# Head output of the first sequence moved among the last attention pairs, and the router worked out for each sequence by itself

## Chip, cores and metric

The kernel runs on one NeuronCore of one Trainium2 chip. The metric is the device time of one execution in microseconds (us), from the median of several runs. Engines are named as the profile names them: PE is TensorE's matmul, PEld its weight load, DVE is VectorE, ACT is ScalarE, POOL is GpSimd and SP issues DMAs.

## What is computed

A two-layer model on x of shape (2, 256, 256), two sequences of 256 tokens. Each layer adds a cross attention over a context of 4096 tokens, then a second block, then a feed-forward block. This case is about the end of the second layer: self attention with 16 heads of 64 (8 causal, 8 not), then a mixture of 8 experts. The last parts of the reference:

```python
out = jnp.concatenate([out_ar, out_diff], axis=1)
out = out.transpose(0, 2, 1, 3).reshape(b, l, H * D_HEAD)
return out @ Wo                       # head output, added to x
...
def _router(x, expert_embeddings):
    dot2 = jnp.einsum('bsh,eh->bse', x, expert_embeddings).reshape(n, E)
    vals, idx = jax.lax.top_k(dot2, K)                  # K = 2 of E = 8
    masked = jnp.full_like(dot2, -jnp.inf).at[rows, idx].set(vals)
    return jax.nn.softmax(masked, axis=-1)
expert_capacity = math.ceil(n_tokens / E * CAP_FACTOR)  # 64
weights = _router(x, expert_embeddings)
ones = (weights > 0).astype(weights.dtype)
cap_ones = jnp.where(jnp.cumsum(ones, axis=0) <= expert_capacity, ones, 0.0)
caw = weights * cap_ones
vals, idx = jax.lax.top_k(caw.T, expert_capacity)
tokens = x_flat[idx.reshape(-1)].reshape(E, expert_capacity, hidden)
inter = jax.nn.relu(jnp.einsum('ech,eih->eci', tokens, first_linear))
out = jnp.einsum('eci,ehi->ech', inter, second_linear) * vals[:, :, None]
final = jnp.zeros((n_tokens, hidden), x.dtype).at[index].add(out.reshape(-1, hidden))
```

The count of chosen tokens (`cumsum`) runs over all 512 tokens, so the second sequence's slots depend on the first sequence's choices. The first sequence's don't depend on the second.

## The kernel before

The 512 tokens lie in four tiles of 128 (X[:, 0] to X[:, 3]). Tiles 0 and 1 are the first sequence (b = 0), 2 and 3 the second. Each engine has one program, written out by hand in order, and the engines meet only at semaphores: an instruction that waits holds up all that stands behind it on its engine. DVE also waits for itself (`done()`) wherever an operation reads the result of the one before it.

**The last pairs of the self attention.** 16 heads of 2 sequences make 16 pairs of heads; pairs 0 to 7 are the first sequence's. PE's loop over pairs does `head_scores(pair + 2)`, two `turn_weights` (transposes, L2618), and `weigh_heads(pair - 1)` (L2642). Before a `turn_weights`, both DVE (`scale_exps`, L1806) and POOL (L763) scale the exponentials. Its result is copied out by DVE (`copy_weights`, L1814) for the even head and by ACT (L1160) for the odd one, and `weigh_heads` reads those copies. The contexts are copied into OT by DVE (`copy_contexts`, L1820) or ACT (`copy_contexts_a`, L1147).

**Head output.** After `weigh_heads(15)` PE multiplies OT by WOM for the four tiles (`linear_rows`, L2186, 8 matmuls a tile, each of float32 and so shown as 2 passes). DVE adds each tile to X (L1843), takes mean and variance (L1419, L1402), adds the epsilon (L1388), has ACT take the square root (L905, which needs the table of the square root), inverts it (L1381) and writes the normalised HLE (`centred`, L1423), all once for each sequence.

**Router.** PE turns HLE (`turn_half`, L2158), ACT copies it (L1019), PE multiplies by the expert embeddings (logits, L2699). With the logits of both sequences in PSUM, DVE makes the choice for four tiles at once (L1858 to L1873), ACT takes one Exp (L1167), DVE ends the choice (L1876 to L1880, CHOSENB for PE), PE counts (L2709), DVE gives slots (L1885, L1888) and builds the selection SEL for each tile (L1891). PE gathers the tokens by a matmul of HLE with SEL that sums over the four tiles (L2717), while DVE works out the shares (L1894 to L1903) and SELW, the weighted selection (L1907, four tiles). PE then waits for the whole SELW and for XG, which ACT copies out (L1170), and goes on with `turn_chosen` (L2729) and the experts (L2738, L2748, L2757) and the combination (L2765), which are left as they are. `keep_awake` (L2166) are matmuls whose result nobody reads; they stand in PE's order where it would wait.

Of the kernel before, what the change touches and what calls it, by code (L numbers as in the profile page):

```python
# [16 lines left out]
P = 128  # L17
# [128 lines left out]
def build(nc, t):  # L146

    ctx = ExitStack()
    with ctx:
# [6 lines left out]
        def f32(at, n):  # L156
            return arena[:, at:at + n]
# [197 lines left out]
        R = [f32(34816 + 32 * i, 32).rearrange("p (t e) -> p t e", e=E) for i in range(12)]  # L355
# [4 lines left out]
        R1 = [f32(35200 + 4 * i, 4) for i in range(8)]  # L360
# [298 lines left out]
        def _(pool):  # L659
# [529 lines left out]
        def _(dve):  # L1189
# [632 lines left out]

            for n in range(4):
                row_maxima(n)
# [3 lines left out]
            for pair in range(16):  # L1828
# [6 lines left out]
                if pair + 1 < 16:  # L1835
                    invert_sums(pair + 1)
                    scale_exps(n + 2)
                copy_weights(n)
                if pair + 1 < 16:
                    scale_exps(n + 3)  # L1840
            copy_contexts(15)
            for b in range(B):
                add_to_x("f_out", 4, lambda i: nc.vector.tensor_tensor(X[:, i, :], X[:, i, :], psum[:, i, 0:256], ALU.add),  # L1843
                         2 * b, 2 * b + 2)
                deviation(first=2 * b, last=2 * b + 2)
                for i in (2 * b, 2 * b + 1):
                    centred(HLE, X, i).then_inc(h_ready, 1)
            dve.wait_ge(on["g_logits"], 1)
            logits, hot1, hot2, weights, chosen, slot, pick = R[0], R[1], R[2], R[3], R[4], R[5], R[6]
            best1, best2, gap, egap, den, share1, share2 = R1[0], R1[1], R1[2], R1[3], R1[4], R1[5], R1[6]  # L1850
            less8 = const("experts").unsqueeze(1).broadcast_to((P, TT, E))

            def over_e(ap):
                return ap.unsqueeze(2).broadcast_to((P, TT, E))

            raw = psum[:, 0, 0:TT * E].rearrange("p (t e) -> p t e", t=TT)
            for best, hot, seen in ((best1, hot1, raw), (best2, hot2, logits)):
                mark(nc.vector.tensor_reduce(best, seen, AX.X, ALU.max))  # L1858
                done()
                mark(nc.vector.tensor_tensor(pick, seen, over_e(best), ALU.is_equal))  # L1860
                done()

                mark(nc.vector.tensor_tensor(pick, pick, less8, ALU.mult))
                done()
                mark(nc.vector.tensor_reduce(R1[7], pick, AX.X, ALU.min))
                done()
                mark(nc.vector.tensor_tensor(hot, less8, over_e(R1[7]), ALU.is_equal))
                done()
                if best is best1:
                    mark(nc.vector.scalar_tensor_tensor(out=logits, in0=hot, scalar=-3.0e38, in1=raw,  # L1870
                                                        op0=ALU.mult, op1=ALU.add))
                    done()
            nc.vector.tensor_tensor(gap, best2, best1, ALU.subtract).then_inc(on["g_logits"], 1)  # L1873

            dve.wait_ge(on["g_logits"], 3)
            mark(nc.vector.scalar_tensor_tensor(out=pick, in0=over_e(egap), scalar=0.0, in1=hot2,  # L1876
                                                op0=ALU.is_gt, op1=ALU.mult))
            done()
            nc.vector.tensor_tensor(CHOSENB, hot1, pick, ALU.add).then_inc(on["g_chosen"], 1)
            mark(nc.vector.tensor_tensor(chosen, hot1, pick, ALU.add))  # L1880
            done()
            dve.wait_ge(on["g_cum"], 1)
            cum = psum[:, 1, 0:TT * E].rearrange("p (t e) -> p t e", t=TT)

            mark(nc.vector.scalar_tensor_tensor(out=slot, in0=cum, scalar=float(CAP), in1=chosen,  # L1885
                                                op0=ALU.is_le, op1=ALU.mult))
            done()
            mark(nc.vector.tensor_tensor(slot, slot, cum, ALU.mult))  # L1888
            done()
            for i in range(TT):  # L1890
                nc.vector.tensor_tensor(SEL[:, i], slot[:, i, :].unsqueeze(2).broadcast_to((P, E, CAP)),  # L1891
                                        const("slots").unsqueeze(1).broadcast_to((P, E, CAP)), ALU.is_equal)\
                  .then_inc(on["g_sel"], 1)
            mark(nc.vector.tensor_scalar(den, egap, 1.0, None, ALU.add))  # L1894
            done()
            mark(nc.vector.reciprocal(share1, den))
            done()
            mark(nc.vector.tensor_tensor(share2, egap, share1, ALU.mult))
            mark(nc.vector.tensor_tensor(hot1, hot1, over_e(share1), ALU.mult))
            done()  # L1900
# [962 lines left out]
```

## Time and profile before

| | before |
|---|---|
| times | 911.25, 912.66, 912.73 us, median 912.66 |
| the profiled execution's own time | 912.04 us |
| span of its trace | 910.2 us |
| PE / DVE / ACT / POOL busy, share of the span | 96% / 67% / 52% / 15% |
| chain that ended last: PE, DVE, ACT | 82%, 10%, 3% |
| TensorE's granted clock, mean | 0.996 of full speed |

The time of the profiled execution is 1.8 us more than the span, which runs from the first to the last instruction that the trace counts as work. Times in the rows further down are from the span's start. A name such as L2186 is a line of the kernel as printed above. A PE busy share of 96% says only that a matmul was almost always under way, keep-awake matmuls among them; whether it was work that the end depends on is read from the chain of waits.

### The profile page before, as it was taken

Reading aid. Unit: us, or ns where it says so; the run is one execution under the profiler, and the core shown is the slowest. Engines: PE = TensorE matmul, PEld = TensorE weight load, DVE = VectorE, ACT = ScalarE, POOL = GpSimd, SP = SyncE. Lnnn points to the kernel's source line nnn. Section 1 sums busy time; section 2 is a strip of 40 time slices with the busy share of each in tenths; the row PEclk is TensorE's granted clock in tenths of the full one; section 3 lists DMA queues with packets and bytes.
Section 4 is the critical chain, followed back from the end, with each engine's and each line's share of the span. In section 5 each row is a group of like instructions: output and inputs, shape, how many; then the busy total and the mean of one; then the engine's idle time right before and its main releaser. Section 6 shows DMA issues by size and latency. Waiting matters only on the chain.

```text
span 910.2 us, 15328 instructions
## 1 busy us (share of the span) xinstructions
PE 874.1 (96%) x6037; PEld 519.5 (57%) x6037; DVE 609.7 (67%) x1068; ACT 474.4 (52%) x958; POOL 136.2 (15%) x141
## 2 busy tenths in 40 slices
PE   7799999999999999999999999999999999999998
PEld 3355544444556665555554578755784784656745
DVE  5879677777886556888883389886724327469352
ACT  4242566777776556777778962314411310668221
POOL 5434011111000000000000071010100005336100
PEclk9899999999999999999999999999999999999999
DMA  9978934546433311333533260084643805000000
GB/s 354 276 202 193 209 110 124 147 125 159 115 71 71 81 36 36 70 71 71 137 123 132 94 249 2 1 277 140 231 185 134 329 1 186 1 1 1 1 1 24
DMA packets 55081, 108.49 MB, mean 119 GB/s; under 512 B 5408, under 2 KB 38176, under 8 KB 49824
## 3 DMA queue, kind: packets, MB, share of 16 engines
q1 hardware_dynamic: 51568, 97.26, 37.6%
q10 hardware_dynamic: 3440, 10.22, 3.7%
q8 instruction: 50, 0.82, 0.4%
q14 instruction: 23, 0.19, 0.1%
HBM read 93.58 MB, written 13.89 MB: 118 GB/s over the span
## 4 chain that ended last, share of the span: by engine, by line
PE 82%; DVE 10%; ACT 3%; issue 2%; DMA 2%; POOL 0%; ACTq 0%; SPq 0%; DVEq 0%
PE psum L2019 14%; PE psum L2001 13%; PE psum L1967 12%; PE psum L2421 6%; PE psum L2449 6%; PE psum L1944 6%; PE psum L2553 5%; PE psum L1934 4%; PE psum L2186 3%; DVE arena L1501 3%; PE psum L2618 2%; DVE arena L1252 2%; PE psum L2603 2%; PE psum L2173 2%; PE psum L2642 1%
## 5 line engine op out<-in xcount | busy, mean ns | idle before, releaser
L1252 DVE TENSOR_REDUCE arena<-psum 128x1 f32<-128x1024 f32 x256 | 301.1, 1219 | 102.4 <-PE psum L1967 101.9
L823 ACT ACTIVATE arena<-psum 128x512 f32<-128x512 f32 x512 | 263.6, 604 | 67.8 <-PE psum L2001 66.5
L1967 PE MATMUL psum<-arena 96*128 96x512 bf16 x512 | 153.2, 381 | 10.0 <-DMA arena<-qparts 4.8
L2001 PE MATMUL psum<-arena 99*128 99x256 bf16 x1024 | 155.1, 274 | 3.9 <-ACT arena L814 1.7
L2019 PE MATMUL psum<-arena 128*32 128x256 f32 x2048 | 137.0, 385 | 0.0
L2001 PEld LDWEIGHTS psum<-arena 99*128 99x128 bf16 x1024 | 80.6, 97 | 98.6 <-ACT arena L823 36.7
L2019 PEld LDWEIGHTS psum<-arena 128*32 128x32 f32 x2048 | 53.4, 109 | 74.2 <-ACT arena L823 30.7
L1934 PE MATMUL psum<-arena 128*128 128x512 f32 x128 | 61.7, 609 | 6.0 <-DMA arena<-ctxT 5.5
L682 POOL TENSOR_TENSOR arena<-arena 128x512 bf16<-128x512 f32 x34 | 41.3, 1214 | 174.5 <-DVE arena L1238 171.8
L1967 PEld LDWEIGHTS psum<-arena 96*128 96x128 bf16 x512 | 48.9, 98 | 29.1 <-DVE arena L1252 11.4
L1944 PE MATMUL psum<-arena 128*128 128x256 f32 x256 | 63.8, 386 | 0.0
L2449 PE MATMUL psum<-arena 128*128 128x256 f32 x256 | 57.9, 379 | 0.0
L2421 PE MATMUL psum<-arena 128*128 128x512 f32 x128 | 57.2, 595 | 0.0
L1944 PEld LDWEIGHTS psum<-arena 128*128 128x128 f32 x256 | 48.5, 194 | 13.1 <-issue 4.8
L2449 PEld LDWEIGHTS psum<-arena 128*128 128x128 f32 x256 | 47.5, 190 | 5.8
L806 ACT ACTIVATE arena<-psum 128x512 f32<-128x512 f32 x32 | 19.1, 598 | 52.4 <-PE psum L1944 52.4
L2173 PE MATMUL psum<-arena 128*128 128x256 f32 (+1 forms) x208 | 44.1, 366 | 0.4 <-ACT arena L1032 0.2
L800 ACT ACTIVATE arena<-psum,arena 128x512 bf16<-128x512 f32 x32 | 22.0, 686 | 42.9 <-PE psum L1934 29.4
L702 POOL MEMSET arena<- 128x4 f32 x1 | 0.1, 106 | 290.1 <-PE psum L2019 290.1
L2553 PE MATMUL psum<-arena 128*128 128x512 f32 x96 | 42.8, 595 | 0.0
L2173 PEld LDWEIGHTS psum<-arena 128*128 128x128 f32 x208 | 37.1, 190 | 7.5 <-issue 1.4
L1934 PEld LDWEIGHTS psum<-arena 128*128 128x128 f32 x128 | 24.0, 195 | 28.3 <-issue 21.6
(269 smaller groups left out, 1014.1 us busy)
## 6 DMA issues: line engine op xcount, KB each, us to landing
kparts<-arena SPq DMA_DIRECT2D x32, 384.0 KB, 3.0
arena<-kparts SPq DMA_DIRECT2D x32, 384.0 KB, 5.2
arena<-kparts SPq DMA_DIRECT2D x32, 256.0 KB, 5.7
arena<-mask SPq DMA_DIRECT2D x8, 1024.0 KB, 5.2
arena<-ctx SPq DMA_DIRECT2D x2, 4096.0 KB, 17.5
arena<-ctxT SPq DMA_DIRECT2D x14, 512.0 KB, 6.0
arena<-ctxT ACTq DMA_DIRECT2D x10, 512.0 KB, 15.4
arena<-mask ACTq DMA_DIRECT2D x4, 1024.0 KB, 9.9
```

Source lines behind the costliest of these rows:

```text
L682: nc.gpsimd.tensor_tensor(parts[:, 2, :], rest, parts[:, 1, :], ALU.subtract).then_inc(k_low, 1)
L823: nc.scalar.activation(PR[step % 4][:, pair * CH:(pair + 1) * CH], exp_bank(step, pair), ACT.Exp)\
L1252: nc.vector.tensor_reduce(MX[g % 2][:, col:col + 1], unit_banks(n).rearrange("p b n -> p (b n)"), AX.X, ALU.max).then_inc(s_maxed, 1)
L1934: last = nc.tensor.matmul(ring_bank(slot), WK[:, k, f * P:(f + 1) * P], CTX[n % SLOTS][:, k, :], start=(k == 0), stop=(k == CT - 1))
L1944: last = nc.tensor.matmul(ring_bank(slot)[:, v * 256:(v + 1) * 256], CTX[n % SLOTS][:, k, (2 * i + v) * P:(2 * i + v + 1) * P], WV[:, k, : ...
L1967: last = nc.tensor.matmul(out, q, KST[g % 2][0:ROWS, quarter, j, half * CH:(half + 1) * CH], start=True, stop=not masked, skip_group_check ...
L2001: last = nc.tensor.matmul(heads[:, u, :], KST[gg % 2][0:KROWS, kc // 8, j, kc % 8 * P:(kc % 8 + 1) * P], QST[0:KROWS, b, G * g + j, :], st ...
L2019: last = nc.tensor.matmul(PV[32 * j:32 * (j + 1), :], V_flat[:, at:at + 32], PR[step % 4][:, j * S:(j + 1) * S], start=(kc == 0), stop=(kc ...
L2173: last = nc.tensor.matmul(out, weights[:, k, m * P:m * P + width], xs[k], start=(k == 0), stop=(k == n - 1))
L2421: last = nc.tensor.matmul(psum[:, unit % 3, :], QC[:, c, w * P:(w + 1) * P], CTXT[w // 2][:, c, n * 512:(n + 1) * 512], start=(c == 0), st ...
L2449: last = nc.tensor.matmul(psum[:, 6, 0:256], PT1[:, k * P:(k + 1) * P], CTXK[w // 2][:, k, :], start=(k == 0), stop=(k == KC - 1), skip_gr ...
L2553: last = nc.tensor.matmul(out, HTF[:, c, i * P:(i + 1) * P], WQKV[which][:, c, half * HALF:(half + 1) * HALF], start=(c == 0), stop=(c == ...
```

## The change

- **Head output of the first sequence.** `heads_out(0)` and `heads_out(1)` stand in PE's loop at pair 14, ahead of `weigh_heads(13)`, and the wait for the first eight pairs' contexts with them. DVE adds them to X at pair 15, ahead of `copy_weights(30)`.
- **Normalisation.** For both sequences the inverse square root is now one power operation on POOL (`power`) instead of ACT's root and DVE's reciprocal.
- **Router for each sequence.** Choice, count, slots, selection and shares are done on two tiles at a time, first for b = 0, then for b = 1. DVE's order becomes: centre 0, last context copy, choose 0, add tiles 2 and 3, ask for the power, slots 0, centre 1, select 0, share 0, choose 1, slots 1, select 1, share 1, then SELW for all four tiles.
- **PE's order** is given at the end of the diff. The keep-awake matmuls go from 8, 3, 14 and 5 to 8, 3, 1 and 5.
- **R and R1**, the router's small tiles, lie elsewhere, since OT is still in use when the first choice is made.

```diff
-        R = [f32(34816 + 32 * i, 32).rearrange("p (t e) -> p t e", e=E) for i in range(12)]
+        R = [f32(55168 + 32 * i, 32).rearrange("p (t e) -> p t e", e=E) for i in range(12)]
...
             nc.gpsimd.tensor_copy(UPPER, const("upper")).then_inc(built, 1)
+            powers[0] += B
+            for b in range(B):
+                power(2 * b, 2 * b + 2)
...
             for b in range(B):
-                root(2 * b, 2 * b + 2)
+                two = slice(2 * b, 2 * b + 2)
                 copy_turned_half(b, HTF)
-            act.wait_ge(on["g_logits"], 2)
-            signal(nc.scalar.activation(R1[3], R1[2], ACT.Exp), "g_logits")
+                act.wait_ge(on["g_logits"], 3 * b + 2)
+                signal(nc.scalar.activation(R1[3][:, two], R1[2][:, two], ACT.Exp), "g_logits")
             for c in range(CT):
...
+            def add_heads(first, last):
+                add_to_x("f_out", 4, lambda i: nc.vector.tensor_tensor(X[:, i, :], X[:, i, :], psum[:, i, 0:256], ALU.add),
+                         first, last)
...
                     scale_exps(n + 2)
+                if pair == 15:
+                    add_heads(0, 2)
+                    ask_root(0, 2)
                 copy_weights(n)
...
-            copy_contexts(15)
-            for b in range(B):
-                add_to_x("f_out", 4, lambda i: nc.vector.tensor_tensor(X[:, i, :], X[:, i, :], psum[:, i, 0:256], ALU.add),
-                         2 * b, 2 * b + 2)
-                deviation(first=2 * b, last=2 * b + 2)
...
+            def centre_for_experts(b):
+                take_power()
                 for i in (2 * b, 2 * b + 1):
                     centred(HLE, X, i).then_inc(h_ready, 1)
...
+            def choose(b):
+                two = slice(2 * b, 2 * b + 2)
+                dve.wait_ge(on["g_logits"], 3 * b + 1)
+                raw, rest, mine = of_bank(0, b), logits[:, two], pick[:, two]
+                for best, hot, seen in ((best1, hot1, raw), (best2, hot2, rest)):
+                    mark(nc.vector.tensor_reduce(best[:, two], seen, AX.X, ALU.max))
...
+                nc.vector.tensor_tensor(gap[:, two], best2[:, two], best1[:, two], ALU.subtract).then_inc(on["g_logits"], 1)
+                dve.wait_ge(on["g_logits"], 3 * b + 3)
+                mark(nc.vector.scalar_tensor_tensor(out=mine, in0=over_e(egap[:, two]), scalar=0.0, in1=hot2[:, two],
+                                                    op0=ALU.is_gt, op1=ALU.mult))
+                done()
+                nc.vector.tensor_tensor(CHOSENB[:, two], hot1[:, two], mine, ALU.add).then_inc(on["g_chosen"], 1)
+                mark(nc.vector.tensor_tensor(chosen[:, two], hot1[:, two], mine, ALU.add))
+                done()
+            def number_slots(b):
+                two = slice(2 * b, 2 * b + 2)
+                dve.wait_ge(on["g_cum"], b + 1)
+                cum = of_bank(1, b)
+                mark(nc.vector.scalar_tensor_tensor(out=slot[:, two], in0=cum, scalar=float(CAP), in1=chosen[:, two],
+                                                    op0=ALU.is_le, op1=ALU.mult))
+                done()
+                mark(nc.vector.tensor_tensor(slot[:, two], slot[:, two], cum, ALU.mult))
+                done()
+            def select(b):
+                for i in (2 * b, 2 * b + 1):
+                    nc.vector.tensor_tensor(SEL[:, i], slot[:, i, :].unsqueeze(2).broadcast_to((P, E, CAP)),
+                                            const("slots").unsqueeze(1).broadcast_to((P, E, CAP)), ALU.is_equal)\
+                      .then_inc(on["g_sel"], 1)
+            def share(b):
+                two = slice(2 * b, 2 * b + 2)
+                mark(nc.vector.tensor_scalar(den[:, two], egap[:, two], 1.0, None, ALU.add))
...
+            centre_for_experts(0)
+            copy_contexts(15)
+            choose(0)
+            add_heads(2, 3)
+            add_heads(3, 4)
+            ask_root(2, 4)
+            number_slots(0)
+            centre_for_experts(1)
+            select(0)
+            share(0)
+            choose(1)
+            number_slots(1)
+            select(1)
+            share(1)
...
+            def heads_out(i):
+                linear_rows(psum[:, i, 0:256], tok(OT, i), WOM, False, "f_out")
+            def logits(b):
+                turned()
+                for i in (2 * b, 2 * b + 1):
+                    for c in range(CT):
+                        last = nc.tensor.matmul(psum[:, 0, i * E:(i + 1) * E], HTF[:, c, i * P:(i + 1) * P], EMB[:, c, :],
+                                                start=(c == 0), stop=(c == CT - 1))
+                last.then_inc(on["g_logits"], 1)
+            def count_chosen(b):
+                pe.wait_ge(on["g_chosen"], b + 1)
+                for i in (2 * b, 2 * b + 1):
+                    for j in range(i + 1):
+                        last = nc.tensor.matmul(psum[:, 1, i * E:(i + 1) * E], UPPER if j == i else ONESB,
+                                                CHOSENB[:, j, :], start=(j == 0), stop=(j == i))
+                last.then_inc(on["g_cum"], 1)
+            def gather(i):
+                pe.wait_ge(on["g_sel"], i + 1)
+                for c in range(CT):
+                    last = nc.tensor.matmul(psum[:, 2 + c, :], HLE[:, i, c * P:(c + 1) * P],
+                                            SEL[:, i].rearrange("p e s -> p (e s)"), start=(i == 0),
+                                            stop=(i == TT - 1), skip_group_check=True)
+                    if i == TT - 1:
+                        last.then_inc(on["g_xg"], 1)
...
+                if pair == 14:
+                    for n in range(8):
+                        contexts_copied(n)
+                    heads_out(0)
+                    heads_out(1)
                 weigh_heads(pair - 1)
             weigh_heads(15)
-            pe.wait_ge(pv_copied, NG + contexts_by(7, True))
-            pe.wait_ge(on["f_pv_copied"], contexts_by(7, False))
-            for i in range(TT):
-                if i == 2:
-                    pe.wait_ge(pv_copied, NG + contexts_by(15, True))
-                    pe.wait_ge(on["f_pv_copied"], contexts_by(15, False))
-                if i == TT - 1:
-                    turn_half(HLE, 0, 4 * TT)
-                linear_rows(psum[:, i, 0:256], tok(OT, i), WOM, False, "f_out")
+            turn_half(HLE, 0, 4 * TT)
+            for n in range(8, 16):
+                contexts_copied(n)
+            heads_out(2)
             pe.wait_ge(on["const_loaded"], 32)
-            for b in range(B):
-                if b:
-                    keep_awake(6, 8)
-                    turn_half(HLE, 1, 4 * TT)
-                    keep_awake(6, 3)
-                turned()
-                for i in (2 * b, 2 * b + 1):
-                    for c in range(CT):
-                        last = nc.tensor.matmul(psum[:, 0, i * E:(i + 1) * E], HTF[:, c, i * P:(i + 1) * P], EMB[:, c, :],
-                                                start=(c == 0), stop=(c == CT - 1))
-            last.then_inc(on["g_logits"], 1)
+            logits(0)
+            heads_out(3)
+            pe.wait_ge(built, 13)
+            count_chosen(0)
+            keep_awake(6, 8)
+            turn_half(HLE, 1, 4 * TT)
+            keep_awake(6, 3)
+            logits(1)
             pe.wait_ge(on["x_ready"], 5 * TT)
-            keep_awake(6, 14)
-            pe.wait_ge(on["g_chosen"], 1)
-            pe.wait_ge(built, 13)
-            for i in range(TT):
-                for j in range(i + 1):
-                    last = nc.tensor.matmul(psum[:, 1, i * E:(i + 1) * E], UPPER if j == i else ONESB,
-                                            CHOSENB[:, j, :], start=(j == 0), stop=(j == i))
-            last.then_inc(on["g_cum"], 1)
+            gather(0)
+            gather(1)
+            keep_awake(6, 1)
+            count_chosen(1)
             keep_awake(6, 5)
-            for i in range(TT):
-                pe.wait_ge(on["g_sel"], i + 1)
-                for c in range(CT):
-                    last = nc.tensor.matmul(psum[:, 2 + c, :], HLE[:, i, c * P:(c + 1) * P],
-                                            SEL[:, i].rearrange("p e s -> p (e s)"), start=(i == 0),
-                                            stop=(i == TT - 1), skip_group_check=True)
-                    if i == TT - 1:
-                        last.then_inc(on["g_xg"], 1)
+            gather(2)
+            gather(3)
             pe.wait_ge(on["g_selw"], TT)
```

## Rows read from the trace of the kernel before

**Rows 1.** Chain that ended last, last 68 us: start us, us, what.
```profile
864.94 1.74 PE psum L2166 x8
868.32 1.07 PE psum L2699 x8
872.78 0.42 PE psum L2709 x10
874.50 7.13 PE psum L2717 x16
```

**Rows 2.** Timeline of PE: start us, us, engine, line, operation, tile, count, [idle before].
```profile
849.63 10.23 PEld L2186 LDWEIGHTS psum<-arena 128*128 128x128 f32 x48 [0.38 <-ACT arena L1147]
863.99 0.95 PE L2699 MATMUL psum<-arena 128*128 128x8 f32 x8
882.43 0.20 PEld L2738 LDWEIGHTS psum<-arena 128*64 128x64 f32 x4 [0.17 <-ACT arena L1170]
```

**Rows 3.** Timeline of the last pairs, PE and VectorE, columns as in the timeline above.
```profile
841.13 1.13 PE L2618 MATMUL psum<-arena 128*128 128x128 f32 x8
845.43 0.63 PEld L2642 LDWEIGHTS psum<-arena 128*64 128x64 f32 x8 [0.17 <-issue]
846.45 0.42 PEld L2618 LDWEIGHTS psum<-arena 128*128 128x128 f32 x4 [0.39 <-DVE arena L1806]
847.14 0.69 DVE L1814 COPY arena<-psum 128x512 f32<-128x512 f32 x1 [0.83 <-PE psum L2618]
847.75 1.49 PEld L2642 LDWEIGHTS psum<-arena 128*64 128x64 f32 x16 [0.17 <-issue]
849.75 0.42 DVE L1820 COPY arena<-psum 128x256 f32<-128x256 f32 x1 [1.92 <-PE psum L2642]
```

**Rows 4.** Timeline of VectorE: adding a head output tile, and one tile's statistics earlier.
```profile
853.39 0.42 DVE L1843 TENSOR_TENSOR arena<-arena,psum 128x256 f32<-128x256 f32 x1 [3.22 <-PE psum L2186]
572.67 0.42 DVE L1483 TENSOR_TENSOR arena<-arena,psum 128x256 f32<-128x256 f32 x1 [1.49 <-PE psum L2186]
573.81 0.15 DVE L1390 TENSOR_SCALAR arena<-arena 128x1 f32<-128x1 f32 x1
```

**Rows 5.** Timeline: powers on POOL and what follows them, and a normalisation before.
```profile
598.89 1.28 DVE L1570 SCALAR_TENSOR_TENSOR arena<-arena 128x1024 f32<-128x1024 f32 x1
599.05 1.52 POOL L737 TENSOR_TENSOR arena<-arena 128x1 f32<-128x1 f32 x1 [2.94 <-DVE arena L1388]
668.20 0.17 DVE L1388 TENSOR_SCALAR arena<-arena 128x2 f32<-128x2 f32 x1
669.18 0.74 DVE L1423 TENSOR_SCALAR arena<-arena 128x256 f32<-128x256 f32 x2 [0.21 <-POOL arena L737]
866.23 0.73 DVE L1423 TENSOR_SCALAR arena<-arena 128x256 f32<-128x256 f32 x2
```

**Rows 6.** Timeline of VectorE: selection, shares, weighted selection.
```profile
873.75 2.50 DVE L1891 TENSOR_TENSOR arena<-arena 128x512 f32<-128x512 f32 x4
876.16 0.16 DVE L1894 TENSOR_SCALAR arena<-arena 128x4 f32<-128x4 f32 x1
877.10 0.19 DVE L1903 TENSOR_TENSOR arena<-arena 128x32 f32<-128x32 f32 x1
877.32 2.50 DVE L1907 TENSOR_TENSOR arena<-arena 128x512 f32<-128x512 f32 x4
```

**Rows 7.** Timeline of ACT: loading the table for the Exp.
```profile
868.28 1.28 ACT L1167 ACT_TABLE_LOAD   x1
```

**Rows 8.** Stretches early on: from:to, length, busy PE PEld DVE ACT POOL, PEclk, DMA.
```profile
37.50:42.30 4.80, 0.00 (x0) 0.00 (x0) 3.62 (x5) 1.26 (x2) 3.35 (x3) 0.77 0.99 230
42.30:46.50 4.20, 4.19 (x10) 2.80 (x11) 2.80 (x4) 0.00 (x0) 0.91 (x2) 0.50 0.77 275
46.90:47.30 0.40, 0.40 (x3) 0.31 (x2) 0.27 (x1) 0.00 (x0) 0.00 (x1) 0.96 1.34 287
97.86:99.52 1.66, 0.00 (x1) 0.01 (x1) 0.00 (x0) 1.15 (x3) 0.00 (x0) 1.00 1.01 201
```

More of the change, by code:

```diff
@@ L359, in build @@
         CHOSENB = b16(44576 + P, TT * E).rearrange("p (t e) -> p t e", e=E)
-        R1 = [f32(35200 + 4 * i, 4) for i in range(8)]
+        R1 = [f32(55552 + 4 * i, 4) for i in range(8)]
         assert 47120 + N_CONSTS <= 48144
@@ L1840, in _ @@
                     scale_exps(n + 3)
-            copy_contexts(15)
-            for b in range(B):
-                add_to_x("f_out", 4, lambda i: nc.vector.tensor_tensor(X[:, i, :], X[:, i, :], psum[:, i, 0:256], ALU.add),
-                         2 * b, 2 * b + 2)
-                deviation(first=2 * b, last=2 * b + 2)
+            logits, hot1, hot2, weights, chosen, slot, pick = R[0], R[1], R[2], R[3], R[4], R[5], R[6]
+            best1, best2, gap, egap, den, share1, share2 = R1[0], R1[1], R1[2], R1[3], R1[4], R1[5], R1[6]
@@ L1849, in _ @@
[L1849 to L1858, printed above, removed]
+            def choose(b):
[5 more added lines that the diff above has]
+                    done()
+                    mark(nc.vector.tensor_tensor(mine, seen, over_e(best[:, two]), ALU.is_equal))
+                    done()
+                    mark(nc.vector.tensor_tensor(mine, mine, less8, ALU.mult))
+                    done()
+                    mark(nc.vector.tensor_reduce(R1[7][:, two], mine, AX.X, ALU.min))
+                    done()
+                    mark(nc.vector.tensor_tensor(hot[:, two], less8, over_e(R1[7][:, two]), ALU.is_equal))
+                    done()
+                    if best is best1:
+                        mark(nc.vector.scalar_tensor_tensor(out=rest, in0=hot1[:, two], scalar=-3.0e38, in1=raw,
+                                                            op0=ALU.mult, op1=ALU.add))
+                        done()
+                nc.vector.tensor_tensor(gap[:, two], best2[:, two], best1[:, two], ALU.subtract).then_inc(on["g_logits"], 1)
+                dve.wait_ge(on["g_logits"], 3 * b + 3)
+                mark(nc.vector.scalar_tensor_tensor(out=mine, in0=over_e(egap[:, two]), scalar=0.0, in1=hot2[:, two],
+                                                    op0=ALU.is_gt, op1=ALU.mult))
@@ L1864, in _ @@
                 done()
-                mark(nc.vector.tensor_reduce(R1[7], pick, AX.X, ALU.min))
+                mark(nc.vector.tensor_tensor(slot[:, two], slot[:, two], cum, ALU.mult))
                 done()
-                mark(nc.vector.tensor_tensor(hot, less8, over_e(R1[7]), ALU.is_equal))
-                done()
[L1869 to L1880, printed above, removed]
@@ L1894, in _ @@
[L1894 to L1900, printed above, removed]
-            mark(nc.vector.tensor_tensor(hot2, hot2, over_e(share2), ALU.mult))
-            done()
-            mark(nc.vector.tensor_tensor(weights, hot1, hot2, ALU.add))
@@ L1904, in _ @@
-            done()
+            def select(b):
[6 more added lines that the diff above has]
+                mark(nc.vector.tensor_scalar(den[:, two], egap[:, two], 1.0, None, ALU.add))
+                done()
+                mark(nc.vector.reciprocal(share1[:, two], den[:, two]))
+                done()
+                mark(nc.vector.tensor_tensor(share2[:, two], egap[:, two], share1[:, two], ALU.mult))
+                mark(nc.vector.tensor_tensor(hot1[:, two], hot1[:, two], over_e(share1[:, two]), ALU.mult))
+                done()
+                mark(nc.vector.tensor_tensor(hot2[:, two], hot2[:, two], over_e(share2[:, two]), ALU.mult))
+                done()
+                mark(nc.vector.tensor_tensor(weights[:, two], hot1[:, two], hot2[:, two], ALU.add))
+                done()
```

20 lines of the change are left out of this document (5 added, 15 removed).

## The prediction

> **What bounds the kernel now.** I first read the page's engine shares: PE is busy for nearly the whole span. That alone says little, since keep-awake matmuls count as busy. So next comes the chain of waits over the last 68 us. Up to the head output it is PE at work. Then it leaves real work: keep-awake matmuls (8 in 1.74 us), logits of the second sequence from 868.32, 3.4 us of small VectorE operations with one Exp between them, the count at 872.78, the selection, and the gather from 874.50 [rows 1]. Behind the gather it is PE's own work to the end. What can be won is therefore the time in which PE waits between the head output and the gather. Then I read the timeline of PE and VectorE over 841 to 883, in which every step below has its row. The point at which both kernels can be compared is the first weight load of the experts, now at 882.43 [rows 2]; all behind it is unchanged. The start is 845.43, where `weigh_heads(13)` begins [rows 3].
>
> **Prices.** A pass of the head output takes 0.2135 us (48 weight loads over 10.23, [rows 2]), so a tile of 16 passes 3.42. `weigh_heads` takes 1.02 (845.43 to 846.45), two of them in a row 1.88 (847.75 to 849.63, the start of the next line) [rows 2, 3]. Two `turn_weights` without a wait between them take 1.13 [rows 3]. Now the last two take 1.30 (846.45 to 847.75), because VectorE and POOL scale late; with 6.8 us of head output ahead of them they no longer wait. Logits of a sequence: 0.95 on PE [rows 2]. From the start of the logits to the count: 4.46 (868.32 to 872.78); from the count to the first gather 1.72 [rows 1]. A gather of two tiles: 8 passes of 0.43, 3.43 (half of the sixteen in 7.13, less the modelled tail) [rows 1].
>
> **Part 1, head output at pair 14.** All adds are to PE's clock of now.
> - Eight waits for contexts stand ahead of `heads_out(0)`. The waits are all met long before, so they cost PE's sequencer only. Four such waits stand before a `weigh_heads`, whose row shows 0.17 idle by issue [rows 3]; twice that, 0.34, is the upper bound, nothing the lower. I take 0.15: start 845.58.
> - Two tiles to 852.42, `weigh_heads(13)` 853.44, two turns 854.57, two `weigh_heads` **856.45**.
> - What VectorE gets ahead of `copy_weights(30)`: its add of tile 1 comes 0.34 behind PE (853.39 against 849.63 + 3.42) [rows 2, 4], at 852.76. From an add to the request for the power one tile takes 1.14 (572.67 to 573.81) [rows 4], the second tile's statistics about 0.43 more: request at 854.33, done by 854.5. The copy takes 0.69 [rows 3] and ends at 855.2. `weigh_heads(15)` wants it at 855.5. So this move past `copy_weights(30)` costs nothing, but by only 0.3 us; if VectorE is later than that, every tenth beyond goes on PE's path.
> - ACT's copy of the odd head stays behind the same transposes as now; it isn't moved.
>
> **Part 2, the power on POOL.** From the request to `centred`, ACT's way and the reciprocal took 0.64 now; POOL's takes 0.98 (668.20 to 669.18) [rows 5]. POOL is idle in this stretch. For the first sequence: 854.33 + 0.98 + 0.74 = 856.1, before `turn_half(0)` wants it at 856.45, so it is hidden (cover 0.4). For the second it is on the path, +0.34. The upper bound is the power that took 1.52 while VectorE ran an operation of 1.28 us on two arena operands [rows 5], 0.8 more than the usual 0.70; here VectorE has two operations of 0.19 there, each with one operand in PSUM, and I take 0.98. This row bears out a rule of the Trainium skill (SBUF — State Buffer, section "SBUF: two separate sides"): VectorE and GpSimd share a port pair, which an operation of VectorE with two SBUF inputs holds to its end while GpSimd is blocked. By that rule alone, with such an operation beside it, the second power would cost 0.8 more; the sum doesn't use it. ACT no longer changes tables; the load of 1.28 us for the Exp (the one for the root is alike) began at 868.28 and was over at 869.56, 3.2 us ahead of the count, which stands a few tenths behind the Exp [rows 1, 7]. Taking both away brings nothing.
>
> **Part 3, the router in halves.** Twelve small operations of the choice are issued twice, the two of the slots and the six of the shares too: 20 more instructions on VectorE, at half the size. An operation on 32 columns takes 0.19, on 4 columns 0.16 [rows 6], so half the size saves about 0.01 each, 0.13 in a choice. So the halves nearly double the time that VectorE spends on the router.
> - `turn_half(0)` from 856.45. `copy_contexts(15)` comes 0.12 behind the last `weigh_heads` and takes 0.42 [rows 3]; then `heads_out(2)` can start, at 857.03, the turn (0.57) is done as well. Ends 860.45. Logits 0 to 861.40, `heads_out(3)` to 864.82.
> - Choice 0 runs beside `heads_out(3)`: count at 860.45 + 4.46 - 0.13 = 864.78. Both sides meet, nothing waits. Count about 0.2.
> - The price of the order: tiles 2 and 3 are added behind choice 0. Tile 2 is ready at 860.8 and waits for VectorE to 864.85. Then each tile passes through add, statistics, aggregate with waits for itself, 1.14 each [rows 4]: request at 867.13, centred from 868.11, and 2.09 from there to logits 1 (866.23 to 868.32) [rows 1, 5]: 870.20. Had tile 2 been taken first, about 0.8 would go.
> - Logits 1 to 871.15, gather of tiles 0 and 1 to 874.58, one keep-awake 0.22 (1.74 / 8, [rows 1]), 874.80. Choice 1 is there at 870.20 + 4.33 = 874.53: hidden by the gather. VectorE before it: centred to 868.85, selection 1.25 (half of 2.50), shares 1.11 (876.16 to 877.32, less 0.05) [rows 6], 871.2: free when the logits come. So here the halves pay: 3.43 of gather lie where 14 keep-awakes were.
> - Count at 874.80, gather of tiles 2 and 3 from + 1.72 = 876.52 to **879.95**. Now the gather ends at 874.50 + 6.86 = 881.36 [rows 1]. Gain there 1.4.
> - But VectorE: selection 1 starts 0.75 before the gather (873.75 against 874.50) [rows 1, 6], 875.77, ends 877.02; shares 1 878.13; the four SELW 2.50 [rows 6]: 880.63. `turn_chosen` waits for all four. Now SELW ends at 879.82, hidden by 1.5 us of gather; then it would be the last, by 0.7. `turn_chosen(0)` from 880.68, the expert load after 1.07 (881.36 to 882.43): **881.75**.
>
> **Sum.** 882.43 - 881.75 = 0.7 us. Against the profiled execution's own time: 912.04 - 0.7 = 911.3. The median of the runs, 912.66, is 0.6 above that execution, so I forecast **912.0** for the median. Most of the 3.4 us of router that becomes hidden is lost again: 0.7 by SELW, about 1 by the later second normalisation, the rest by waits that the keep-awakes only covered.
>
> **Rivals.**
> - **The gather stays last.** VectorE's waits for itself are shorter, or the contexts' waits cost nothing, so SELW is ready before the gather ends. For it: VectorE needs to be only 0.7 faster over 20 operations and four waits, and the serial add of tiles 2 and 3 is priced from a row of another stage. Against: each price is from a row. The gain is then the 1.4 at the gather's end, and up to 2.5 if the serial adds take 0.5 each less: 910.2 to 911.3, in the middle 910.7. Chance 0.2.
> - **Eaten up.** POOL's power takes 1.52 beside VectorE (+0.5), the waits 0.34 (+0.2), halves are no shorter (+0.2), `copy_weights(30)` comes late. Gain about nothing, 912.7 (to 913.3). Chance 0.17.
> - **The clock falls, slower.** After the count of sequence 0 PE has 8 keep-awakes, to 865.05 + 1.74 = 866.8, and then nothing until `turn_half(1)` at 868.11 + 0.53 = 868.6: a pause of 1.85 us; now keep-awakes and work fill almost all of it. In this trace a pause of 1.66 left the clock full, one of 4.80 had it fall to half (1.2 of 2.4 GHz), and half it stayed for 4.6 us after work had begun again, 42.30 to 46.90 [rows 8]. It decides from a pause nearer to the second than to the first. If the clock falls, the next 4.6 us do 2.3 of work: 2.3 lost, net +1.6: 914.3. 1.85 lies close to the harmless row, so 0.05. More generally slower by other late steps (several tenths each of parts 1 and 3 in a row) 0.03.
> - **It doesn't do what it says**, as when PE reaches `heads_out(0)` with contexts not copied: those of pairs 0 to 7 are copied long before pair 14. No chance worth a number.
>
> **How the numbers follow.** Forecast (gain 0.3 to 1.6) 0.55, gather last 0.2, eaten up 0.17, slower 0.08. The range takes in the first three with the scatter of the runs (1.5 us between lowest and highest): 910.1 to 913.6. A measurement of this kernel can tell about 0.2%, 1.8 us, from no change. Faster by more than that needs most of the second case or a median that falls well: 0.2. Slower by more: 0.08, the clock and late steps, 0.1 with scatter. The same: 0.7.
>
> **What would show it.** PE at `turn_half(0)` near 856.4 with no gap in front of `weigh_heads(15)`; `heads_out(3)` directly followed by the count; request to `centred` 0.98 for both sequences; a PE pause of near 1.9 us ahead of `turn_half(1)` with PEclk 1.00; VectorE's last SELW later than the last gather matmul by about 0.7, `turn_chosen` released by VectorE; the expert load 0.7 earlier. It is wrong if `copy_weights(30)` releases PE, if small operations on 16 columns differ much from those on 32, or if SELW isn't last.

## The result, and the profile after

| | before | after |
|---|---|---|
| median of 22 runs | 913.02 us | 914.77 us |
| lowest, highest | 911.25, 914.36 | 912.05, 916.08 |
| profiled execution's own time, span | 912.04, 910.2 | 914.01, 912.1 |
| TensorE's granted clock, mean | 0.996 | 0.994 |

The ratio is 1.0017 with a 95% interval of 1.0010 to 1.0024: the changed kernel is slower, by 1.75 us between the medians and 1.6 us by the ratio, a little less than 0.2%. The forecast was 0.7 us faster. The runs after are spread in an odd way: two of the 22 took 912.1 us at a mean clock of 0.996, two took 912.6 and 913.2 at 0.994, and the other 18 lie at 914.0 to 916.1 with a clock of 0.993 or 0.994. The profiled execution is one of the 18.

In the kernel after, `linear_rows` is L2225, `turn_half` L2197, `keep_awake` L2205, the logits L2702, the count L2710, the gather L2717, `turn_chosen` L2780, the first products of the experts L2789; on VectorE `centred` is L1426, the selection L1912, SELW L1946. First the windows over the router in the trace after, in the form of [rows 8]: from:to, length, busy time of PE, PEld, DVE, ACT and POOL, then PEclk.

```profile
866.50:868.40 1.90, 0.17 (x1) 0.00 (x0) 1.20 (x7) 0.00 (x0) 0.69 (x1) 1.00 0.00 0
868.40:869.50 1.10, 1.06 (x6) 0.71 (x7) 1.10 (x3) 0.18 (x1) 0.00 (x0) 0.83 0.00 0
869.50:871.00 1.50, 1.50 (x8) 1.08 (x6) 1.16 (x7) 0.41 (x1) 0.00 (x0) 0.50 0.00 0
871.00:873.00 2.00, 2.00 (x7) 1.48 (x8) 0.65 (x4) 0.00 (x0) 0.00 (x0) 0.50 0.04 8
873.00:875.00 2.00, 2.00 (x4) 0.82 (x3) 1.46 (x10) 0.20 (x1) 0.00 (x0) 0.50 0.02 4
875.00:876.00 1.00, 1.00 (x2) 0.34 (x1) 0.40 (x3) 0.00 (x0) 0.00 (x0) 0.52 0.00 0
876.00:877.00 1.00, 1.00 (x4) 0.42 (x3) 0.00 (x0) 0.00 (x0) 0.00 (x0) 1.00 0.00 0
```

PEclk is the third number from the end. It is still 1.00 while PE pauses (0.17 us of work in 1.90), falls just after work has begun again, stays at 0.50, which is 1.2 of 2.4 GHz, from about 869 to 876, and is full again after. PE reads as busy all through: half speed looks like work. PE's timeline says what ran there:

```profile
868.44 0.78 PE L2197 MATMUL psum<-arena 128*128 128x128 f32 x4 [1.77 <-DVE arena L1426]
870.25 1.71 PE L2702 MATMUL psum<-arena 128*128 128x8 f32 x8
871.82 5.73 PE L2717 MATMUL psum<-arena 128*128 128x512 f32 x8
877.60 0.32 PE L2710 MATMUL psum<-arena 128*128 128x8 bf16 x7
879.19 3.70 PE L2717 MATMUL psum<-arena 128*128 128x512 f32 x8 [0.17 <-DVE arena L1912]
880.75 2.50 DVE L1946 TENSOR_TENSOR arena<-arena 128x512 f32<-128x512 f32 x4
883.30 1.09 PE L2780 MATMUL psum<-arena 128*128 128x128 f32 x8 [0.41 <-DVE arena L1946]
884.32 1.94 PE L2789 MATMUL psum<-arena 128*64 128x512 f32 x8
```

The brackets of the first line give the pause, 1.77 us, and who ended it: VectorE's `centred` for the second sequence. The logits (L2702) took 1.71 instead of 1.07 for the same eight passes [rows 1], and the gather of tiles 0 and 1 took 5.73 where the same work on tiles 2 and 3 at full clock takes 3.70. That gather hid the second choice in the forecast; now it delays the count, to 877.4.

So that traces can be compared although their earlier stages differ by some tenths of a us, the text below measures one **distance**: from the start of `turn_weights(28)`, the transposes whose wait for POOL is 0.67 or 0.68, to the first weight load of the experts. Before it is 843.95 to 882.43, 38.48 us; after, 843.77 to 884.32, 40.55. The starting rows, the kernel before first:

```profile
843.95 0.63 PE L2618 MATMUL psum<-arena 128*128 128x128 f32 x4 [0.67 <-POOL arena L763]
843.77 0.63 PE L2657 MATMUL psum<-arena 128*128 128x128 f32 x4 [0.68 <-POOL arena L763]
```

### The profile page after: what moved, and what is told of

Same layout as the page of the kernel before. It is cut to its first block, busy times and chain, and to the rows that moved or that the text cites. A ratio compares the mean times of both kernels' runs of the same rounds, so it can differ in the third digit from the quotient of the medians.

```text
span 912.1 us, 15333 instructions
## 1 busy us (share of the span) xinstructions
PE 873.7 (96%) x6024; PEld 519.4 (57%) x6024; DVE 612.9 (67%) x1089; ACT 471.9 (52%) x955; POOL 137.8 (15%) x143
## 4 chain that ended last, share of the span: by engine, by line
PE 80%; DVE 11%; issue 3%; ACT 3%; DMA 2%; POOL 0%; ACTq 0%; POOLq 0%; SPq 0%; DVEq 0%
PE psum L2058 14%; PE psum L2040 13%; PE psum L2006 11%; PE psum L2460 6%; PE psum L2488 6%; PE psum L1983 6%; PE psum L2592 5%; PE psum L1973 4%; DVE arena L1504 3%; PE psum L2225 3%; DVE arena L1255 2%; PE psum L2642 2%; PE psum L2657 2%; PE psum L2212 2%; PE psum L2472 1%
```

## The experiments

**Theory 1, the clock:** the pause lets the clock fall, and without that the change wins what was forecast. **Rival, the work:** VectorE's doubled small operations and the later second normalisation cost more than was forecast. The table gathers all kernels that were run. The pause and the distance are those of the one profiled execution; the ratio is to the kernel before on the same chip, measured beside it.

| kernel | PE's pause in the router, us | distance, us | median, us | ratio (95% interval) |
|---|---|---|---|---|
| before | 0.37 | 38.48 | 913.0 | 1 |
| after | 1.77 | 40.55 | 914.77 | 1.0017 (1.0010 to 1.0024) |
| fill15 | 0.27 | 37.57 | 912.45 | 0.9993 (0.9984 to 1.0002) |
| fill12 | 0.91 | 37.56 | 912.19 | 0.9996 (0.9986 to 1.0007) |
| none0 | 3.52 | 41.34 | 915.96 | 1.0030 (1.0021 to 1.0039) |
| before_no14 | 3.46 | 39.51 | 914.21 | 1.0014 (1.0005 to 1.0023) |
| before_6 | 2.10 | 39.71 | 914.25 | 1.0015 (1.0005 to 1.0025) |
| part1_only | 0.45 | 38.81 | 913.73 | 1.0007 (0.9998 to 1.0016) |
| fill_t2first | none | 37.19 | 912.14 | 0.9987 (0.9979 to 0.9996) |
| t2first_11 | 0.2 | 36.84 | 911.71 | 0.9984 (0.9975 to 0.9993) |
| t2first_11_tw | 0.2 | 36.51 | 911.29 | 0.9980 (0.9971 to 0.9989) |
| t2_10_tw_root | none | 36.20 | 911.10 | 0.9977 (0.9968 to 0.9986) |

### Filling the pause

```diff
             count_chosen(0)
-            keep_awake(6, 8)
+            keep_awake(6, 15)
```

> The changed kernel with 15 keep-awake matmuls instead of 8 ahead of the turn of the second sequence, so that PE's pause of 1.8 us there (866.7 to 868.4 in the changed kernel's trace) is filled; nothing else differs. Theory 1, the clock: the pause lets the clock fall to half in most executions and the loss is that. Then PEclk is 1.00 from 860 to the end, the gather of tiles 0 and 1 takes 0.43 a pass instead of 0.85, and the time is that of the changed kernel's two shortest runs, 912.1, so 0.5 to 1.2 below the kernel before (ratio 0.9987 to 0.9995) with all runs within 1.5 us. Rival, the work: the loss comes from VectorE's doubled small operations and the later normalisation of the second sequence. Then the time stays at 914 to 915, since the matmuls in the pause touch none of that.

All 11 runs lie at 911.6 to 913.0, and the distance is 37.57: 0.91 less than before and 2.98 less than after. Seven matmuls whose result nobody reads bring 2.3 us in the median (914.77 to 912.45). In its trace:

```profile
844.57 0.63 PE L2657 MATMUL psum<-arena 128*128 128x128 f32 x4 [0.67 <-POOL arena L763]
869.24 0.78 PE L2197 MATMUL psum<-arena 128*128 128x128 f32 x4 [0.27 <-DVE arena L1426]
870.77 1.06 PE L2702 MATMUL psum<-arena 128*128 128x8 f32 x8
871.68 3.68 PE L2717 MATMUL psum<-arena 128*128 128x512 f32 x8
877.00 3.70 PE L2717 MATMUL psum<-arena 128*128 128x512 f32 x8 [0.17 <-DVE arena L1912]
878.57 2.50 DVE L1946 TENSOR_TENSOR arena<-arena 128x512 f32<-128x512 f32 x4
881.12 1.09 PE L2780 MATMUL psum<-arena 128*128 128x128 f32 x8 [0.41 <-DVE arena L1946]
882.14 1.94 PE L2789 MATMUL psum<-arena 128*64 128x512 f32 x8
```

But for the seven matmuls these are the same instructions in the same order. The first gather takes 3.68 again, and VectorE does its work as it did. The rival falls: VectorE's operations are all there, and the kernel is no slower than the one before.

### Making it longer, and making one in the kernel before

`none0` takes the eight matmuls away instead; `before_no14` takes the 14 under the router out of the kernel before; `before_6` leaves 6 of these.

```diff
             count_chosen(0)
-            keep_awake(6, 8)
             turn_half(HLE, 1, 4 * TT)
...
             pe.wait_ge(on["x_ready"], 5 * TT)
-            keep_awake(6, 14)
+            keep_awake(6, 6)
```

(The first part is none0's, the second before_6's; before_no14 has no line in place of the 14.)

> The changed kernel without the 8 keep-awake matmuls there: the pause grows from 1.8 to about 3.6 us. Theory 1, the clock: it falls in every execution, none at 912; the median is as in the changed kernel or up to 1 us longer, 914.8 to 915.8, as the fall comes earlier but what it costs is bounded by the time until it rises. Rival, the work: 914.8, and the runs spread as they did, with some at 912.

> The kernel before without its 14 keep-awake matmuls under the router: PE pauses about 3.4 us ahead of the count, all else as it was. Theory 1, the clock: in the kernel before these matmuls hold the clock, which the halves' order gives up in part. Then it falls to half here and the gather behind it takes up to twice 6.9 us: 915 to 917. Rival: nobody reads these matmuls and the chain of waits runs over VectorE there, so the time stays at 912.7 to 913.2.

> The kernel before with 6 keep-awake matmuls under the router instead of 14: a pause of about 1.7 to 2.1 us ahead of the count, of the length of the one in the changed kernel, at another place. If the pause's length alone decides, the clock falls in most runs and costs 1.5 to 2.5 as in the changed kernel: 914 to 915.5. If what PE does after it counts too (here five keep-awakes and a gather without waits follow, in the changed kernel a turn, a wait and logits), it falls in few or none: 912.9 to 913.5.

`none0`: all ten runs at 914.8 to 916.8, the median 1.2 above the changed kernel's where at most 1 was expected. The clock is at half from about 868.2, still within the pause, to 878.5, and the distance is 3.8 longer than in fill15. `before_no14`: 912.9 to 916.0, median 1.3 above before, which is less than the 2 to 4 us expected. Its lowest run, 912.85 with a mean clock of 0.996, looks as if the clock had held even through this pause (no trace of it was taken). `before_6` has a shorter pause and loses as much, as was expected if the pause's length decides. Here are windows of `before_6`, and then PE's timeline of it:

```profile
871.00:873.00 2.00, 0.42 (x2) 0.00 (x0) 1.49 (x9) 0.20 (x1) 0.00 (x0) 1.00 0.00 0
873.00:874.00 1.00, 0.48 (x11) 0.37 (x12) 0.49 (x3) 0.01 (x1) 0.00 (x0) 0.91 0.00 0
875.00:876.00 1.00, 1.00 (x4) 0.63 (x3) 1.00 (x3) 0.00 (x0) 0.00 (x0) 0.50 0.03 8
877.00:878.00 1.00, 1.00 (x3) 0.40 (x3) 0.86 (x6) 0.00 (x0) 0.00 (x0) 0.88 0.00 0
```

```profile
873.52 0.41 PE L2709 MATMUL psum<-arena 128*128 128x8 bf16 x10 [2.10 <-DVE arena L1879]
875.86 7.72 PE L2717 MATMUL psum<-arena 128*128 128x512 f32 x16
```

L2709 is the count, L2717 the gather, L1879 VectorE's choice for PE. The fall comes just after work has begun again, as in the kernel after, and lasts 3.4 us instead of 6.8. Much of it lies on keep-awake matmuls and on the time in which VectorE builds the selection, so that only part of it reaches the path (the gather begins at + 2.34 behind the count where it was 1.72, [rows 1], and takes 7.72 instead of 7.13). So the 14 matmuls of the kernel before are worth about 1.3 us, and the change took 13 of them away where its gather fills the time, but left a new hole at another place. That the fall came with 2.10 at this place, with keep-awake matmuls right ahead of the pause and the count and more of them right behind it, says that it isn't peculiar to the changed order.

### A pause of half the length

```diff
             count_chosen(0)
-            keep_awake(6, 8)
+            keep_awake(6, 12)
```

> The changed kernel with 12 keep-awake matmuls instead of 8 ahead of the turn of the second sequence: a pause of about 0.9 us where the changed kernel has 1.8, fill15 none and none0 3.6. Theory: a pause of 0.9 leaves the clock full in all runs, as pauses of 1.1 to 1.7 early in the trace did: 912.3 to 912.6, as fill15. Rival: already 0.9 lets it fall in some runs, since keep-awakes ahead and a nearly idle PE behind add to it: a spread from 912 to 915.

```profile
868.91 0.78 PE L2197 MATMUL psum<-arena 128*128 128x128 f32 x4 [0.91 <-DVE arena L1426]
```

Seven of ten runs lie at 910.3 to 912.3 with a clock of 0.996 or more, three at 913.8, 914.0 and 914.4 with 0.994. The profiled one is of the seven and its clock is 1.00 all through this stage. The spread is the one that this run's rival named, but that the three fell at this pause isn't shown: no trace of one of them was taken, and a time near 914 with a mean clock of 0.994 doesn't say where the clock fell. `t2first_11`, further down, shows that. Its profiled execution took 914.03 us at 0.994, though its router ran at full clock with a pause of 0.2. It fell far earlier, behind a pause that stands in every kernel here, and that is the 1.66 us of [rows 8]:

```profile
101.24 0.61 PE L2040 MATMUL psum<-arena 99*128 99x256 bf16 x4 [1.67 <-ACT arena L817]
```

```profile
102.00:102.50 0.50, 0.50 (x6) 0.27 (x4) 0.18 (x1) 0.50 (x2) 0.00 (x0) 1.00 0.88 148
102.50:103.00 0.50, 0.50 (x3) 0.20 (x2) 0.50 (x1) 0.50 (x2) 0.00 (x0) 0.52 0.92 201
103.00:105.00 2.00, 2.00 (x8) 1.06 (x7) 1.77 (x2) 1.63 (x4) 0.00 (x0) 0.50 1.07 202
```

So the forecast's harmless row isn't always harmless: all twelve traces have this pause, 1.67 us in each, and in one of them the clock fell 1.3 us behind it and stayed at half for 3.4 us. For fill12 that leaves a comparison: of the 56 runs of the five kernels with a pause of 0.3 or less, this one alone lies over 913.2; of fill12's ten, three do. That speaks for falls at 0.91, but doesn't show them. With 1.77, 18 of 22 runs lie high, with 3.52 (none0) all ten.

### Which part wins

The kernel before with the head output of the first two tiles at pair 14, their adds ahead of `copy_weights(30)` and both powers on POOL as in the change; the router and the keep-awakes stay as before:

```diff
+                if pair == 14:
+                    for n in range(8):
+                        contexts_copied(n)
+                    for i in range(2):
+                        linear_rows(psum[:, i, 0:256], tok(OT, i), WOM, False, "f_out")
                 weigh_heads(pair - 1)
             weigh_heads(15)
+            turn_half(HLE, 0, 4 * TT)
...
+                if pair == 15:
+                    add_to_x("f_out", 4, ..., 0, 2)
+                    ask_root(0, 2)
                 copy_weights(n)
```

> The kernel before with the head output of the first sequence at pair 14, its adds ahead of the last weights' copy, and both normalisations by POOL's power, but with the router for all four tiles at once and all 14 keep-awake matmuls. Theory 1: moving the head output alone wins nothing, because PE was at work there anyhow; only the 0.2 of wait ahead of the last turns goes, and POOL's power puts 0.3 on the second sequence's way: 0 to +0.4 us against the kernel before (ratio 0.9998 to 1.0006). Rival: the early head output is what wins in the filled kernel (0.9 between common points); then this one is 0.5 to 1 us below the kernel before.

The distance is 38.81, 0.33 more than before, and the median is 0.6 more (interval from 0.2 less to 1.5 more). Moving the head output moves work from one full stretch of PE to another, and POOL's power lies on the second sequence's way, as in the change (the move was not run without the power). What it does is to give the first sequence's choice its place beside `heads_out(3)`; the 0.9 us of fill15 come with the halves. That the halves need the early head output as their condition follows from the order; no run had them without it.

### What the forecast said was lost, taken back piece by piece

fill_t2first is fill15 with the first change below. t2first_11 has 11 keep-awakes in place of 15. t2first_11_tw has the second change besides, and t2_10_tw_root, with 10 keep-awakes, the third, on VectorE, with `root(2, 4)` ahead of `copy_turned_half(1, HTF)` on ACT and no `power(2, 4)` on POOL.

```diff
             copy_contexts(15)
-            choose(0)
             add_heads(2, 3)
+            choose(0)
             add_heads(3, 4)
...
-            pe.wait_ge(on["g_selw"], TT)
...
                 for i in range(TT):
+                    pe.wait_ge(on["g_selw"], i + 1)
                     last = nc.tensor.transpose(psum[:, k % 2, i * P:(i + 1) * P],
...
             def centre_for_experts(b):
-                take_power()
+                take_root(2, 4) if b else take_power()
```

> As fill15, and VectorE adds tile 2 and takes its statistics ahead of the first choice, not behind it. Tile 2 is ready 0.5 us before the logits; the first choice moves back by about 0.6, which the head output of tile 3 hides but for 0.5; only tile 3 is left between the first choice and the request. The request for the power should come 0.4 to 0.6 earlier than in fill15 and the expert load as much, if the second normalisation is on the path as forecast: 0.3 to 0.6 us less than fill15. If VectorE's queue decides instead (first choice late, all behind it late), no gain over fill15 or up to 0.3 loss.

> As fill_t2first with 11 keep-awake matmuls in place of 15. In fill_t2first the request comes 0.7 earlier, but 15 matmuls last past it and hold back the turn of the second sequence by 0.5. With 11 the turn should begin 0.53 behind the start of the centring. Theory 1: PE is free in time, clock stays at 1.00 in all runs: 0.4 to 0.6 less than fill_t2first, near 911.6, ratio 0.998 to 0.9987. Rival: the matmuls that are too many cost nothing, as VectorE's later queue decides; then as fill_t2first.

> As t2first_11, and PE waits ahead of each transpose of the weighted selection for that tile alone, not for all four first. If VectorE's last SELW is what releases PE (0.4 behind the gather's end in fill15), three of the four transposes go ahead and only the last waits: 0.3 less than t2first_11. If the added waits cost as much as they save: no difference.

> As t2first_11_tw with 10 keep-awake matmuls, and the second sequence's inverse square root by ACT's root and VectorE's reciprocal again in place of POOL's power. If 0.64 against 0.98 from request to centring holds here too, 0.3 less than t2first_11_tw. If loading the table of the root and then that of the Exp again (1.28 each), which the halves put between two Exps, doesn't fit beside other work, 1 to 2.5 us more.

The steps shorten the distance by 0.38, 0.35, 0.33 and 0.31, as was expected but for the second, which was to bring at least 0.4. In the medians a single step is lost in the intervals; from fill_t2first on the kernels are faster than the one before beyond theirs. For fill15 against the kernel before (0.9984 to 1.0002) that rests on the distance; against the kernel after the intervals don't touch. In fill_t2first 15 keep-awakes outlast VectorE, whose request comes 0.7 earlier, so half of the gain waits for t2first_11. In the last kernel the table of the root is loaded once more and that of the Exp once more, and this is how that lies (L1393 is the request, L907 ACT's root, L1428 the centring, L1172 the second Exp):

```profile
865.91 1.28 ACT L907 ACT_TABLE_LOAD   x1
867.62 0.17 DVE L1393 TENSOR_SCALAR arena<-arena 128x2 f32<-128x2 f32 x1
867.82 0.20 ACT L907 ACTIVATE arena<-arena 128x2 f32<-128x2 f32 x1 [0.63 <-DVE arena L1393]
868.33 0.74 DVE L1428 TENSOR_SCALAR arena<-arena 128x256 f32<-128x256 f32 x2
870.38 1.28 ACT L1172 ACT_TABLE_LOAD   x1
874.40 0.20 ACT L1172 ACTIVATE arena<-arena 128x2 f32<-128x2 f32 x1 [2.74 <-DVE arena L1890]
```

Both loads are over before what needs them is asked for (867.19 against 867.82, 871.66 against 874.40), and from the request to the centring it is 0.71 (867.62 to 868.33) against 1.04 in t2first_11. The Trainium skill (ScalarE: Activation LUTs, section "What ACT_TABLE_LOAD costs") puts a load at 1.28 us, which these rows show too; its further 1.38 for a drain shows nowhere here. From the end of the first Exp (865.89) to the root lie 1.93 us, less than both together, and the root began on its operand's arrival. Neither is on the path. This last kernel is the fastest: 911.10 against 913.15 beside it, ratio 0.9977 (0.9968 to 0.9986), 2 us below the kernel before.

## Why the prediction was wrong, point by point

The forecast's sum can be laid against the traces stage by stage, as distances from `turn_weights(28)` (843.95 in its clock, 843.77 after, 844.57 in fill15):

| | forecast | after | fill15 |
|---|---|---|---|
| `turn_half(0)` | 12.50 | 12.37 | 12.37 |
| logits 0 | 16.50 | 16.37 | 16.37 |
| request for the second power | 23.18 | 23.06 | 23.06 |
| `turn_half(1)` | 24.69 | 24.64 | 24.64 |
| logits 1 | 26.25 | 26.19 | 26.20 |
| count of the second sequence | 30.85 | 33.62 | 30.69 |
| gather of tiles 2 and 3 | 32.57 | 35.42 | 32.43 |
| first load of the experts | 37.80 | 40.55 | 37.57 |

- **Head output at pair 14: right.** `copy_weights(30)` came in time, no gap stood ahead of `weigh_heads(15)`. The eight waits cost nothing at `heads_out(0)`; 0.33 of issue showed behind the tiles, at `weigh_heads(13)`, which was not forecast and whose cause isn't shown. (The 0.17 of issue was read as that of four waits; `weigh_heads` has three.)
- **POOL's power: right**, 1.01 and 1.05 from request to centring for 0.98; it was not held up by VectorE's two small operations. ACT's tables: right, and the last experiment shows the loads hidden even where they are doubled.
- **The router in halves: right.** Operations on 16 columns came every 0.21 us, on 32 every 0.22. There are 23 more of them, not 20, as the choice has fifteen and not twelve; the sum doesn't use the count. The second choice took 4.49 to the count instead of 4.33, so in fill15 VectorE and not the gather releases the count, at 30.69 where 30.85 was forecast. The second normalisation cost what was said: fill_t2first and t2first_11 took back 0.73 together.
- **SELW last: right**, but PE waits 0.41 for it in fill15 and not 0.7. The gain is 0.91 instead of 0.68: 0.13 of the difference stands in the table at `turn_half(0)` already, nearly all the rest behind the last gather.
- **The clock: wrong, and this alone turned the sign.** The step that failed is in the third rival: the pause was worked out well, at 1.85 us against 1.77, but its chance was put at 0.05 with "1.85 lies close to the harmless row". A single harmless pause of 1.66, read from one trace, was taken as a rule. The trace of the kernel after shows the fall behind 1.77, the times of 18 of its 22 runs say that it was the usual case, and in another trace the harmless pause itself was followed by a fall. The price was too low as well: 2.3 lost was forecast from 4.6 us at half, while the half lasted 6.8 us and cost 2.98 in the profiled execution (the gather 2.05 of it, the logits 0.65). [rows 8] had this number: a mean of 0.77 over the pause of 4.80 puts the fall at about 40.1, so there too the half lasted 6.8 us, of which 2.2 lay in the pause. In the kernel after all of it lay on work. The net of that rival, 914.3, is close to the measured 914.77, partly by luck, since its price and the gain set against it were both too small.
- The range ended at 913.6, because with 0.05 the rival was left outside. What the runs give is a chance of about 0.8 (18 of 22), and with it the forecast is slower; one pause that held and one that didn't give no ground for 0.05, and already with a fifth the range should have reached 914.3.
- The list of what would show the steps asked for "PEclk 1.00" over the pause. PEclk is 1.00 over the pause and falls only behind it; the sign to look for was the windows after it.
- The Trainium skill (TensorE: Matmul & The Clock Gate, section "🎯 Why this matters for your kernels") warns of idle gaps as well, but from a length above all pauses here but none0's and before_no14's. By it the clock would have fallen neither in the changed kernel (1.77) nor in before_6 (2.10) nor in t2first_11 (1.67), and in all three traces it did. The measurement decides.

**Open.** Two of 22 runs seem to have kept their clock through the same pause; no trace of such a run was taken. The earlier pause of 1.67 shows in traces that one and the same pause can go either way (11 held, one fell), but not what decides. Nor is it shown how much the emptier stretches around the pause, against its length alone, add to the fall.

## What to carry to other kernels

When a change takes waiting time away from one place, look where PE will now pause, and price each new pause as a possible fall of the clock. The shortest behind which a trace here shows one is 1.67 us; at 0.91 a fall isn't shown, but three slow runs of ten speak for it. The work behind is then priced at half speed, for 3.4 to 10.2 us in these traces, and the chance isn't read from one pause that went well. Cheap matmuls that nobody reads close such a hole, but only as many as fit: too many hold up the work behind them, as 15 did where 11 were enough. A move that only shifts PE's work within a full stretch won nothing by itself here; it can pay if another engine's chain gets cover by it.

## What the runs showed of the hardware that was not expected

- The clock fell with pauses of 1.77 us (after), 2.10 (before_6), and 3.5 (none0, before_no14), in the first two and in before_no14 only when work had begun again or was about to, in none0 2 us into the pause, and not at all in the profiled executions with 0.91 (fill12) and 0.27 (fill15).
- The same pause of 1.67 us, at 98 to 102 us in all twelve traces, was followed by a fall in one (t2first_11, 1.3 us after it ended) and by none in eleven, [rows 8] among them.
- The time at half differed: 6.8 us in the kernel after, 3.4 in before_6, in before_no14 and in t2first_11, 10.2 in none0. So the price of a fall can't be taken from one other fall.
- The eight waits for contexts, long met, cost PE nothing that shows at their place: after them the head output began 0.45 us behind the last transposes' load (844.67 to 845.12), no more than the 0.58 of `weigh_heads` in their place before. Whether the 0.33 of issue ahead of `weigh_heads(13)` is theirs isn't shown.
